# Output bias added by DMA from tile 2 on, and moves in VectorE's order, in a fused state-space and feed-forward layer

## The chip, the cores and the metric

The kernel runs on one core of one Trainium2 chip. The metric is the device time of one execution in microseconds; three runs of the kernel before took 1415.86, 1417.70 and 1417.96 us, so their median is 1417.7 us.

## The reference, cut to what matters

The input is x of 8192 rows by 512 columns, in float32. LN is a normalisation of each row without weights.

```
x = x + LN(attn(LN(x)))
x = x + LN(ffn(LN(x)))

attn(r):  u, v = split(r @ in_w + in_b);  v = conv3(silu(v)) + conv_b
          h_t = a*h_(t-1) + b*v_t;  y = c*h + d*v            (a scan over all 8192 rows)
          h = (u*silu(y)) @ out_w + out_b + r                (out_b: the output bias)
          return LN(h)*ln_w + ln_b
ffn(r):   W1, W2 rounded to -1, 0, 1
          return gelu(r @ W1 + b1) @ W2 + b2                 (2048 wide inside)
```

## The kernel before, in words

The rows are cut into 16 tiles of 512, each of four blocks of 128 rows (index j). Step s of a software pipeline works on four tiles at once: the feed-forward of tile fa = s-2, the second half of attention of tile c = s-1, the first half of attention of tile n = s+1, and the end of tile e = s-3. Steps 0 to 2 are the start-up, written out by hand; `for s in LATER` runs steps 3 to 17. Matmul operands are split into a high and a low float16 part, and each projection is three matmuls. For tiles 2 to 12 (`seven(t)`), the second matrix of the feed-forward uses seven half-width products in place of eight. These need differences of weight blocks (`combined`, made by eight calls of `combine(q, g)` in step 3) and, for each pair of chunks, four sums of the low parts (`presums`, L969 to L976, on VectorE).

The engines' queues are in order, and every order is written by hand: a list of (position, work) pairs is sorted by position and emitted by `run`. The names AT_... hold positions. A position of j means about "beside chunk j of the feed-forward" (16 chunks in a step, nine in the first half and seven in the second). What the step does on each engine:

- TensorE: `f1` of chunks 0 to 8 with `f2` four chunks behind, then `in_proj("u", c)` of four blocks (L579 to L581), three `f2`, `o(c, j)` of four blocks (L593 to L595), `in_proj("v", n)` of two blocks, the other `f1` and `f2`, and two more blocks of v. The u, o and v groups take turns in two PSUM banks (`misc`), so each group waits until the reader of the group before last is done: `gate` for u, `h_add` for o, `silu_v` for v. The first v group of a step also waits for the four transposing DMAs of x1T (L471), which SyncE issues once `t_lo("t1", n, j)` is done.
- VectorE: the ending of tile e (`epilogue`: additions `f_add` L938, statistics `f_stats` L907, `aggr` L917), `taps`, `scan` L1088, `y` L1098, `lo` L925 and `presums`. Then the four `gate` (L1120), statistics of x, `gate_lo`, `t_lo` (L1133), `h_add` (L1144), and the normalisations of tile c (`norms`).
- ScalarE: `gelu` L1855, `hi` L1869, `ffn_norm(e, j)` L1880 (it waits for GpSimd's `rstd_f(e)`, L2292 to L2324, which waits for the `aggr` of tile e), `silu_y` L1921, `gate_hi`, and then for each j `front(n, j)` and `residual(c, j)` L1916. The last writes the normed x into hb.
- GpSimd: the small vectors of each normalisation, `finish(e, j)` L2339 (a DMA that adds a block to the output in device memory), `keep_state`, and `add_bias(c, j)` L2349: it waits for `residual(c, j)` and adds the bias row to hb. `h_add(c, j)` waits for this and adds the product of the out projection.

The diff touches the positions at the top, `epilogue`, `h_add`, the loop body of VectorE, one line of ScalarE's loop and `add_bias`.

Of the kernel before, what the change touches and what calls it, by code (L numbers as in the profile page):

```python
# [24 lines left out]
P = 128  # L25
# [28 lines left out]
AT_F_ADD, AT_F_STATS, AT_F_AGGR = 0.0, 0.8, 1.15  # L54
AT_F_NORM = (4.15, 4.2, 5.15, 5.2)
AT_TAP0, AT_TAP2 = (1.1, 1.15, 1.4, 1.45), (1.3, 1.35, 2.25, 2.26)
AT_SCAN, AT_Y = (2.3, 2.35, 3.4, 3.45), (3.3, 3.35, 4.3, 4.35)
AT_LO = (1.2, 2.2, 2.32, 2.38, 3.36, 4.2)
AT_D_CONV, AT_CENTRE = (3.15, 3.16, 4.15, 4.16), (13.3, 13.5, 14.3, 14.5)
AT_NORMS, AT_NORMS_LAST = 7.7, 0.5  # L60
# [11 lines left out]
AT_TAP0_NEXT = (17.41, 17.42, 17.43, 17.44)  # L72
AT_PRESUM, AT_PRESUM_LAST = .005, .01
AT_F_STATS_SEVEN = 2.27
AT_F_NORM_SEVEN = (6.15, 6.2, 7.15, 7.2)
AT_COMBINED = (7.65, 9.25, 11.65, 14.65, 17.5)
LAG_END = 5
TH = TT // 2
AT_V = (8.9, 8.95, 16.3, 17.2)
# [16 lines left out]
def spread(at, step, works):  # L96

    return [(at + step * i, w) for i, w in enumerate(works)]


def build(nc, x, w_in, w_out, w1t, w2t, params, rows, out):
# [20 lines left out]
    def seven(t):  # L122

        return 1 < t < NT - 3
# [19 lines left out]
    with ExitStack() as ctx:  # L144
# [3 lines left out]
        def sem(name):  # L148
            return ctx.enter_context(nc.semaphore(name))
# [106 lines left out]
        out_st = [sem(f"out_st{i}") for i in range(NB)]  # L256
        x1_st = [sem(f"x1_st{i}") for i in range(NB)]
        last_st = [sem(f"last_st{i}") for i in range(NB)]

        const_ok, prep, pmx, pm1, scale_ok = sem("const_ok"), sem("prep"), sem("pmx"), sem("pm1"), sem("scale_ok")  # L260
        win_h, win_l, wo_h, wo_l = sem("win_h"), sem("win_l"), sem("wo_h"), sem("wo_l")
# [629 lines left out]
        def _(ve_):  # L891
# [17 lines left out]
            def aggr(ln, t, j):  # L909
                ve_.wait_ge(bn_ok[ln], NB * t + j + 1)  # L910
                if ln == 0 and t in (1, 2):
                    ve_.wait_ge(front_rs, min(j, 2) + 1 if t == 1 else NB + j // 2)
                elif ln == 0 and t > 2:
                    ve_.wait_ge(rs_ok[0], t - 2)
                elif t > 0:
                    ve_.wait_ge(rs_ok[ln], t)
                ve_.bn_aggr(mean_var(ln)[:, j, :], raw_stats(ln)[:, j, :]).then_inc(mv_ok[ln], 1)  # L917
# [11 lines left out]
            def f_add(e, j):  # L929
                if e == NT - 1 and j >= 2:  # L930
                    ve_.wait_ge(f2_sum, j - 1)
                elif j % 2 == 0:
                    ve_.wait_ge(f2_mm, half_done(e, j // 2))
                if e + 1 < NT - 1:
                    ve_.wait_ge(x3_lo, NB * (e + 1) + j + 1)
                else:
                    ve_.wait_ge(out_st[j], 16 * e)
                ve_.scalar_tensor_tensor(out=hb[:, j, :], in0=f2b[j][:, :], scalar=f_inv[:, 0:1], in1=b2_row,  # L938
                                         op0=ALU.mult, op1=ALU.add).then_inc(f_ok, 1)

            def f_stats(e, j):
                ve_.wait_ge(f_ok, NB * e + j + 1)
                stats(4, e, j, fo(e, j))
# [93 lines left out]
            def epilogue(e):  # L1037
                if seven(e):
                    return (spread(AT_F_ADD, .1, drain(e, 1))
                            + spread(AT_F_STATS_SEVEN, .001, [lambda j=j: f_stats(e, j) for j in range(2, NB)])  # L1040
                            + spread(AT_F_STATS_SEVEN + .004, .001, [lambda j=j: aggr(4, e, j) for j in range(2, NB)]))
                return (spread(AT_F_ADD, .2, [lambda j=j: f_add(e, j) for j in range(NB)])
                        + spread(AT_F_STATS, .1, [lambda j=j: f_stats(e, j) for j in range(NB)])
                        + spread(AT_F_AGGR, .01, [lambda j=j: aggr(4, e, j) for j in range(NB)]))

            def x_stats(n, j):

# [87 lines left out]

            def h_add(c, j):
                ve_.wait_ge(o_mm, NB * c + j + 1)
                if c > 0:
                    ve_.wait_ge(resb_ok, NB * (c - 1) + j + 1)
                else:  # L1140
                    ve_.wait_ge(x1_hi, j + 1)
                    ve_.wait_ge(wo_sc_ok, 2)
                dst = hb_of(c)[:, j, :]
                ve_.scalar_tensor_tensor(out=dst, in0=bank("o", c, j)[:, :], scalar=o_inv[:, 0:1],  # L1144
                                         in1=dst, op0=ALU.mult, op1=ALU.add).then_inc(h_ok, 1)
# [575 lines left out]
            for s in LATER:  # L1721
# [17 lines left out]
                    continue  # L1739
                if c is not None and c > 0:  # L1740
                    gate(c, 0)
                    gate(c, 1)
                if s == 3:
                    combine(2, 0)
                if n is not None:
                    run(ln1(n))
                if s == NT - 1:
# [9 lines left out]
                parts = drain(fa, 0) if seven(fa) else []  # L1757
                if n is not None:
                    if s == 3:
                        combine(0, 0)  # L1760
                    t_lo("t1", n, 0)
                    if s == 3:
                        combine(0, 1)
                    t_lo("t1", n, 1)
                    for part in parts[:3]:
                        part()
                    t_lo("t1", n, 2)
                    h_add(c, 0)
                    for part in parts[3:4]:
                        part()  # L1770
                    t_lo("t1", n, 3)
                    parts = parts[4:]
# [27 lines left out]
                    items = norms(c)  # L1800
                if s == 3:
                    b2_difference()
                    items += [(at, lambda i=i: combine(*divmod(i, 2))) for i, at in zip((2, 3, 5, 6, 7), AT_COMBINED)]
                if s < NT - 1:
                    items += [(at, lambda b=b: taps(s, b, True)) for b, at in enumerate(AT_TAP0_NEXT)]
                if fa is not None:
# [37 lines left out]
        def _(act):  # L1844
# [32 lines left out]
            def ffn_norm(e, j):  # L1877
                if j == 0:
                    act.wait_ge(rs_ok[4], e + 1)
                act.activation(fo(e, j), fo(e, j), ACT.Identity, bias=nm4[:, j:j + 1],  # L1880
                               scale=rs4[:, j:j + 1]).then_inc(fn_ok, 1)
# [345 lines left out]
            for s in LATER:  # L2227
                fa, c, n, e = tiles(s)
                items = []
                if e is not None:  # L2230
                    items += [(at, lambda j=j: ffn_norm(e, j)) for j, at in enumerate(AT_F_NORM_SEVEN if seven(e) else AT_F_NORM)]
                if c is not None and s < NT:
                    items += [(at, lambda b=b: d_conv(c, b)) for b, at in enumerate(AT_D_CONV)]
                if fa is not None:
                    items += ffn(fa, range(half(s)))
                if s == NT:
                    items += [(at, lambda j=j: t_hi("t3", c, j)) for j, at in enumerate(AT_T3_HI_LAST)]
                if s == NT + 1:
                    items += [(at, lambda j=j: last_norm(j)) for j, at in enumerate(AT_FIRST_LAST_NORM)]
                run(items)  # L2240
                if s >= NT:
                    continue
                for b in range(KC):
                    silu_y(c, b)
                if s == NT - 1:
                    centre_tap(NT - 1, 0)
                    centre_tap(NT - 1, 1)
                for b in range(KC):
                    gate_hi(c, b)
                    if s == NT - 1 and b < 2:  # L2250
                        centre_tap(NT - 1, 2 + b)
                for j in range(NB):
                    if n is not None:
                        front(n, j)
                    residual(c, j)
                if s == NT - 1:
                    for b in range(KC):
                        d_conv(NT - 1, b)
                    for j in range(NB):
                        residual(NT - 1, j)  # L2260
                items = ffn(fa, range(half(s), FC)) if fa is not None else []
                if n is not None:
                    items += [(at, lambda b=b: silu_v(n, b)) for b, at in enumerate(AT_V)]
                if s < NT - 1:
                    items += [(at, lambda b=b: centre_tap(s, b)) for b, at in enumerate(AT_CENTRE)]
                if c is not None:
                    items += [(at, lambda j=j: t_hi("t3", c, j))
                              for j, at in enumerate(AT_T3_HI if s < NT - 1 else AT_T3_HI_PAIR)]
                if s == NT - 1:
                    items += [(AT_SILU_LAST, lambda b=b: silu_y(NT - 1, b)) for b in range(KC)]  # L2270
                    items += [(AT_GATE_HI_LAST, lambda b=b: gate_hi(NT - 1, b)) for b in range(2)]
                run(items)
                if s == NT - 1:
                    for b in range(2, KC):
                        gate_hi(NT - 1, b)
# [4 lines left out]
        def _(pool):  # L2280
# [65 lines left out]
            def add_bias(c, j):  # L2346
                pool.wait_ge(res_ok, NB * (c - 1) + j + 1)
                dst = hb_of(c)[:, j, :]
                pool.tensor_tensor(dst, dst, ob_row, ALU.add).then_inc(resb_ok, 1)  # L2349

            def edges(n):

# [173 lines left out]
```

## Time and profile before

| What | Value |
|---|---|
| Runs | 1415.86, 1417.70, 1417.96 us |
| The profiled execution's own time | 1419.9 us |
| Its span, first to last instruction | 1418.1 us |
| TensorE busy | 1391.3 us (98% of the span) |
| VectorE, ScalarE, GpSimd busy | 1210.6, 911.7, 369.4 us |
| Mean granted TensorE clock | 0.997 |

Busy time is the union of the intervals in which an engine executed something. "Idle before" a row is the idle time of that engine right ahead of it, and the arrow tells which instruction's signal ended it. The profiled execution's own time is 1.8 us over its span, and 2.2 us over the median of the runs.

### The profile page before, as it was taken

The numbers are of one execution on the slowest core, as the hardware profiler recorded it, in microseconds if no ns is written. First come the engines' busy times: TensorE is split into PE (matmuls) and PEld (weight loads), VectorE is DVE, ScalarE is ACT, GpSimd is POOL, SyncE is SP. The second block draws the span as 40 slices with busy tenths as digits, with TensorE's granted clock in tenths as the row PEclk, the third lists the DMA queues.
The fourth block names the chain that finished last, engine by engine and source line by source line (L and its number), as shares of the span: only waits on it lengthen the run. The fifth ranks groups of instructions, "written<-read, shape, count | busy, mean of one in ns | idle before, by whom it ended". The sixth has DMA issues, their size and how long they took to land.

```text
span 1418.1 us, 24900 instructions
## 1 busy us (share of the span) xinstructions
PE 1391.3 (98%) x8954; PEld 878.9 (62%) x8954; DVE 1210.6 (85%) x2360; ACT 911.7 (64%) x1504; POOL 369.4 (26%) x522
## 2 busy tenths in 40 slices
PE   6999999999999999999999999999999999999997
PEld 4444556657667575666757667575676757555664
DVE  7999988978889898898988889898898988898534
ACT  7998565656757566666656757566666656854543
POOL 4234142321312213132231312214122231313111
PEclk9999999999999999999999999999999999999999
DMA  8713431513305133141332315133041332202320
GB/s 230 254 51 79 116 80 25 120 30 81 55 16 119 31 90 60 21 99 31 97 53 68 63 21 119 30 90 60 16 105 31 91 59 60 31 1 60 60 31 31
DMA packets 164652, 98.12 MB, mean 69 GB/s; under 512 B 133680, under 2 KB 133680, under 8 KB 164400
## 3 DMA queue, kind: packets, MB, share of 16 engines
q1 hardware_dynamic: 155888, 80.79, 22.8%
q0 software_dynamic: 8640, 15.73, 8.1%
q8 instruction: 71, 1.16, 0.3%
q14 instruction: 53, 0.43, 0.1%
HBM read 31.49 MB, written 32.51 MB: 45 GB/s over the span
## 4 chain that ended last, share of the span: by engine, by line
PE 52%; DVE 21%; issue 12%; ACT 4%; POOL 3%; DMA 0%; DVEq 0%; ACTq 0%; POOLq 0%
PE f1b L617 6%; PE f1b L616 6%; PE misc L581 5%; PE misc L580 5%; PE misc L579 5%; PE f2b L667 4%; DVE ring L925 4%; PE f2b L657 4%; DVE vl L1079 3%; PE misc L593 3%; PE misc L595 3%; PE misc L594 3%; PE f2b L640 3%; PE f2b L642 3%; DVE bn L907 2%
## 5 line engine op out<-in xcount | busy, mean ns | idle before, releaser
L616 PE MATMUL f1b<-x3T,w 128*128 128x256 f16 x1792 | 399.1, 273 | 0.0
L617 PE MATMUL f1b<-x3T,w 128*128 128x256 f16 x1792 | 399.0, 273 | 0.0
L1855 ACT ACTIVATE ring<-f1b,par 128x256 f32<-128x256 f32 x480 | 201.4, 471 | 212.5 <-PE f1b L617 212.2
L2292 POOL TENSOR_SCALAR ve<-mv 128x4 f32<-128x4 f32 (+2 forms) x89 | 46.5, 523 | 764.3 <-DVE mv L917 764.3
L925 DVE SCALAR_TENSOR_TENSOR ring<-ring,f_sc 128x512 f16<-128x512 f32 x256 | 187.2, 737 | 60.2 <-ACT ring L1869 60.1
L616 PEld LDWEIGHTS f1b<-x3T,w 128*128 128x128 fp8e5 x1792 | 175.7, 98 | 25.0 <-issue 0.4
L617 PEld LDWEIGHTS f1b<-x3T,w 128*128 128x128 fp8e5 x1792 | 175.6, 98 | 24.4
L1869 ACT ACTIVATE ring<-ring,f_sc 128x512 f16<-128x512 f32 x256 | 182.2, 719 | 0.0
L657 PE MATMUL f2b<-w,ring 128*128 128x512 fp8e5 x704 | 180.7, 379 | 0.0
L579 PE MATMUL misc<-x1T,win_hi 128*128 128x512 f16 x456 | 172.8, 379 | 0.0
L581 PE MATMUL misc<-x1T,win_lo 128*128 128x512 f16 x456 | 172.8, 379 | 0.0
L580 PE MATMUL misc<-x1T,win_hi 128*128 128x512 f16 x456 | 172.8, 379 | 0.0
L1984 ACT ACTIVATE vb<-misc,par,inv_sig 128x512 f32<-128x512 f32 x54 | 41.9, 776 | 116.2 <-PE misc L581 116.0
L907 DVE BATCH_NORM_STATS2 bn<-hb 128x6 f32<-128x512 f32 x162 | 104.7, 677 | 0.2
L2349 POOL TENSOR_TENSOR hb<-hb,row 128x512 f32<-128x512 f32 x56 | 79.7, 1425 | 91.4 <-ACT hb L1916 91.4
L657 PEld LDWEIGHTS f2b<-w,ring 128*128 128x128 f16 x704 | 68.9, 98 | 50.2
L640 PE MATMUL f2b<-w,ring 128*128 128x512 fp8e5 x256 | 97.0, 379 | 0.9 <-DVE ring L925 0.8
L642 PE MATMUL f2b<-w,ring 128*128 128x512 fp8e5 x256 | 97.0, 379 | 0.0
L1079 DVE SCALAR_TENSOR_TENSOR vl<-vb,par,vl 128x512 f32<-128x512 f32 x128 | 92.4, 769 | 1.0 <-POOL vb L2398 0.8
L593 PE MATMUL misc<-wo_hi,g_hi 128*128 128x512 f16 x240 | 91.0, 379 | 2.2 <-DVE hb L1144 1.8
L594 PE MATMUL misc<-wo_lo,g_hi 128*128 128x512 f16 x240 | 91.0, 379 | 0.0
L595 PE MATMUL misc<-wo_hi,g_lo 128*128 128x512 f16 x240 | 91.0, 379 | 0.0
(263 smaller groups left out, 2693.5 us busy)
## 6 DMA issues: line engine op xcount, KB each, us to landing
out_dram<-xs SPq DMA_DIRECT2D x60, 256.0 KB, 3.0
xs<-x_dram SPq DMA_DIRECT2D x14, 1024.0 KB, 5.9
out_dram<-hb POOLq DMA_DIRECT2D x38, 256.0 KB, 5.3
out_dram<-stage POOLq DMA_DIRECT2D x22, 256.0 KB, 4.7
ring<-w1t_dram SPq DMA_DIRECT2D x3, 1024.0 KB, 13.4
stage<-w2t_dram SPq DMA_DIRECT2D x3, 1024.0 KB, 7.9
x1T<-tp SPq DMA_TRANSPOSE x68, 3.1
xs<-x_dram SPq DMA_DIRECT2D x4, 256.0 KB, 3.5
```

The lines of the kernel that those rows point to most:

```text
L579: pe.matmul(o[:, :], wh, x1T[:, s_, k, :], start=k == 0, stop=False)
L580: pe.matmul(o[:, :], wh, x1T[:, s_, KC + k, :], start=False, stop=False)
L581: mm = pe.matmul(o[:, :], wl, x1T[:, s_, k, :], start=False, stop=k == KC - 1)
L616: pe.matmul(o_, w, src[:, k, h * TH:(h + 1) * TH], start=k == 0, stop=False)
L617: mm = pe.matmul(o_, w, src[:, KC + k, h * TH:(h + 1) * TH], start=False, stop=k == KC - 1)
L640: pe.matmul(f2b[q][:, :], h_hi[:, i % H_SLOTS, qs], w2[:, chunk, :], start=chunk == 0, stop=False)
L642: mm = pe.matmul(f2b[q][:, :], h_lo[:, i % H_SLOTS, qs], w2[:, chunk, :], start=False, stop=chunk == FC - 1)
L657: pe.matmul(f2b[q][:, :], h_hi[:, r, n * TH + q * P:n * TH + (q + 1) * P], w2[:, chunk, :], start=p == 0 and n == 0, stop=False, skip_grou ...
L925: ve_.scalar_tensor_tensor(out=h_lo[:, i % H_SLOTS, :], in0=gg[:, i % G_SLOTS, :], scalar=f_sc[:, 0:1], in1=h_hi[:, i % H_SLOTS, :], op0=A ...
L1079: ve_.scalar_tensor_tensor(out=dst, in0=src, scalar=w, in1=dst, op0=ALU.mult, op1=ALU.add).then_inc(done, 1)
L1855: ins = act.activation(gg[:, i % G_SLOTS, ts], f1b[i % 2][:, ts], ACT.Gelu, bias=par[:, B1 + chunk:B1 + chunk + 1], scale=1.0 / ACT_SCALE)
L1869: act.activation(h_hi[:, i % H_SLOTS, :], gg[:, i % G_SLOTS, :], ACT.Copy, scale=f_sc[:, 0:1]).then_inc(hh_ok, 1)
```

## The change

From tile 2 on, `add_bias` no longer adds on GpSimd. GpSimd issues a DMA that reads the bias row from device memory for all 128 partitions and adds it to the block in hb, and `h_add` waits for the landing of this DMA, by new semaphores `ob_in`. Tile 1 keeps the addition on GpSimd.

In VectorE's order: `scan` of block 3 moves from position 3.45 to 4.25 in every step. The eight `combine` of step 3 move up by one place each, so that none is left at position 17.5. In the one step whose tile e comes right before the tiles of the seven products (step 4, e = 1), the statistics of tile e move from 0.8 to 2.4, and ScalarE's `ffn_norm` of this tile from the positions 4.15 to 5.2 to the positions 6.15 to 7.2.

```diff
-AT_SCAN, AT_Y = (2.3, 2.35, 3.4, 3.45), (3.3, 3.35, 4.3, 4.35)
+AT_SCAN, AT_Y = (2.3, 2.35, 3.4, 4.25), (3.3, 3.35, 4.3, 4.35)
...
+AT_F_STATS_NEXT = 2.4
...
-AT_COMBINED = (7.65, 9.25, 11.65, 14.65, 17.5)
+AT_COMBINED = (7.65, 9.25, 11.65, 14.65)
...
+        ob_in = [sem(f"ob_in{i}") for i in range(NB)]
...
+                at = AT_F_STATS_NEXT if seven(e + 1) else AT_F_STATS
                 return (spread(AT_F_ADD, .2, [lambda j=j: f_add(e, j) for j in range(NB)])
-                        + spread(AT_F_STATS, .1, [lambda j=j: f_stats(e, j) for j in range(NB)])
-                        + spread(AT_F_AGGR, .01, [lambda j=j: aggr(4, e, j) for j in range(NB)]))
+                        + spread(at, .1 if at == AT_F_STATS else .001, [lambda j=j: f_stats(e, j) for j in range(NB)])
+                        + spread(at + .004 if seven(e + 1) else AT_F_AGGR, .01 if at == AT_F_STATS else .001,
+                                 [lambda j=j: aggr(4, e, j) for j in range(NB)]))
...
             def h_add(c, j):
                 ve_.wait_ge(o_mm, NB * c + j + 1)
-                if c > 0:
-                    ve_.wait_ge(resb_ok, NB * (c - 1) + j + 1)
+                if c > 1:
+                    ve_.wait_ge(ob_in[j], 16 * (c - 1))
+                elif c == 1:
+                    ve_.wait_ge(resb_ok, j + 1)
...
                 if c is not None and c > 0:
                     gate(c, 0)
+                    if s == 3:
+                        combine(2, 0)
                     gate(c, 1)
                 if s == 3:
-                    combine(2, 0)
+                    combine(0, 0)
...
                     if s == 3:
-                        combine(0, 0)
+                        combine(0, 1)
                     t_lo("t1", n, 0)
                     if s == 3:
-                        combine(0, 1)
+                        combine(1, 0)
                     t_lo("t1", n, 1)
...
-                    items += [(at, lambda i=i: combine(*divmod(i, 2))) for i, at in zip((2, 3, 5, 6, 7), AT_COMBINED)]
+                    items += [(at, lambda i=i: combine(*divmod(i, 2))) for i, at in zip((3, 5, 6, 7), AT_COMBINED)]
...
-                    items += [(at, lambda j=j: ffn_norm(e, j)) for j, at in enumerate(AT_F_NORM_SEVEN if seven(e) else AT_F_NORM)]
+                    items += [(at, lambda j=j: ffn_norm(e, j)) for j, at in enumerate(AT_F_NORM_SEVEN if seven(e) or seven(e + 1) else AT_F_NORM)]
...
             def add_bias(c, j):
                 pool.wait_ge(res_ok, NB * (c - 1) + j + 1)
                 dst = hb_of(c)[:, j, :]
-                pool.tensor_tensor(dst, dst, ob_row, ALU.add).then_inc(resb_ok, 1)
+                if c == 1:
+                    pool.tensor_tensor(dst, dst, ob_row, ALU.add).then_inc(resb_ok, 1)
+                    return
+                if c > 2:
+                    pool.wait_ge(ob_in[j], 16 * (c - 2))
+                pool.dma_start(dst, rows[0:1, :].partition_broadcast(P)[:, 0, :], accum_op=ALU.add).then_inc(ob_in[j], 16)
```

## Rows read from the trace of the kernel before

**Rows 1.** The page, part 1: busy us, share of span, instructions.
```profile
PE 1391.3 (98%) x8954; PEld 878.9 (62%) x8954; DVE 1210.6 (85%) x2360; ACT 911.7 (64%) x1504; POOL 369.4 (26%) x522
```

**Rows 2.** TensorE's waits: line, releaser, us in total, times, longest.
```profile
PE f2b L667 <- DVE stage L969: 2.6, 1, 2.6
PE misc L593 <- DVE hb L1144: 1.8, 1, 1.8
```

**Rows 3.** Timeline of VectorE, turn to step 4: start us, us, line, idle before.
```profile
259.08 1.22 DVE L955 TENSOR_TENSOR stage<-w,stage 128x1024 fp8e5<-128x1024 fp8e5 x1
...
262.85 2.46 DVE L907 BATCH_NORM_STATS2 bn<-hb 128x6 f32<-128x512 f32 x4
```

**Rows 4.** Timeline of TensorE: the first f2 of step 4, and of step 6.
```profile
265.74 1.03 PE L657 MATMUL f2b<-w,ring 128*128 128x512 fp8e5 x4
269.32 0.52 PE L667 MATMUL f2b<-w,ring 128*128 128x256 fp8e5 x2 [2.56 <-DVE stage L969]
...
273.51 1.03 PE L657 MATMUL f2b<-w,ring 128*128 128x512 fp8e5 x4
...
440.54 1.03 PE L657 MATMUL f2b<-w,ring 128*128 128x512 fp8e5 x4
...
443.91 1.03 PE L657 MATMUL f2b<-w,ring 128*128 128x512 fp8e5 x4
```

**Rows 5.** Windows: stretch, length, busy by engine, granted clock, DMA share, GB/s.
```profile
268.00:274.00 6.00, 4.67 (x26) 3.37 (x27) 5.93 (x11) 4.56 (x9) 2.70 (x5) 0.72 0.31 42
126.00:130.00 4.00, 3.16 (x15) 1.48 (x16) 4.00 (x11) 0.54 (x2) 2.79 (x5) 1.00 0.67 245
```

**Rows 6.** Timelines of step 6: the ending of tile 3, and the first gate.
```profile
443.29 0.30 DVE L917 BATCH_NORM_AGGREGATE mv<-bn 128x2 f32<-128x6 f32 x2
...
447.43 0.27 POOL L2324 TENSOR_SCALAR nm<-tmp 128x4 f32<-128x4 f32 x1
...
448.26 1.41 DVE L1098 SCALAR_TENSOR_TENSOR yb<-vl,cb_par,yb 128x512 f32<-128x512 f32 x2
...
448.83 1.51 ACT L1880 ACTIVATE stage<-stage,nm,rs 128x512 f32<-128x512 f32 x2
451.12 0.84 ACT L1855 ACTIVATE ring<-f1b,par 128x256 f32<-128x256 f32 x2 [0.78 <-PE f1b L617]
...
459.13 0.75 DVE L1120 SCALAR_TENSOR_TENSOR yb<-misc,bu_sig,yb 128x512 f32<-128x512 f32 x1 [0.35 <-ACT yb L1921]
...
461.10 0.38 PE L579 MATMUL misc<-x1T,win_hi 128*128 128x512 f16 x1
```

**Rows 7.** Timelines of step 6: bias additions, `h_add`, out projection, first v block.
```profile
470.31 1.27 POOL L2349 TENSOR_TENSOR hb<-hb,row 128x512 f32<-128x512 f32 x1 [3.07 <-ACT hb L1916]
477.00 1.28 POOL L2349 TENSOR_TENSOR hb<-hb,row 128x512 f32<-128x512 f32 x1 [0.95 <-ACT hb L1916]
...
481.72 0.75 DVE L1144 SCALAR_TENSOR_TENSOR hb<-misc,o_inv,hb 128x512 f32<-128x512 f32 x1
...
476.34 0.38 PE L593 MATMUL misc<-wo_hi,g_hi 128*128 128x512 f16 x1
...
481.52 0.38 PE L579 MATMUL misc<-x1T,win_hi 128*128 128x512 f16 x1
```

**Rows 8.** DMA views, 440 to 465 us: software queue, landings of adding DMAs.
```profile
q0 software_dynamic: 576, 1.05, 30.2%
...
out_dram<-stage POOLq DMA_DIRECT2D x2, 256.0 KB, 4.6
```

**Rows 9.** DMA views, 465 to 490 us: hardware queue, transposes, last issue.
```profile
q1 hardware_dynamic: 4224, 1.05, 26.5%
...
x1T<-tp SPq DMA_TRANSPOSE x4, 3.1
...
476.97 1.23 SPq L471 DMA_TRANSPOSE x1T<-tp  x1
```

**Rows 10.** The page, part 6: plain loads of 1 MB.
```profile
xs<-x_dram SPq DMA_DIRECT2D x14, 1024.0 KB, 5.9
```

## The prediction

> **What bounds the kernel now.** I read the page's first part, then TensorE's waits, then timelines of the two places where the change could bite. TensorE is busy in 1391.3 of 1418.1 us [rows 1], so only a change in what TensorE waits for moves the time. All its waits in the steady part come to one entry: 2.6 us, once, until a VectorE sum (L969) is done [rows 2]. The other one shown, 1.8 us, lies in the start-up at 126 us, which the change doesn't touch. The reader is to see where the 2.6 us lie: at 265.74 us TensorE starts the first f2 of step 4, and it goes on only at 269.32 [rows 4]. From this f2 to the next one takes 273.51 - 265.74 = 7.77 us; the same stretch of step 6 takes 443.91 - 440.54 = 3.37 us. So this place costs 4.40 us, more than the wait: the granted clock is 0.72 in 268 to 274 us [rows 5], full speed for a part and half for the rest, so after the wait TensorE ran at 1.2 GHz for a while. The 1.8 us wait left the clock at 1.00 in 126 to 130 us [rows 5]. I keep this pair: waits of 1.8 us cost themselves, one of 2.6 us cost 1.7 us more.
>
> **The moves around step 4.** Ahead of these sums VectorE's list has a combine at 259.08 (1.22 us, some 1.13 to the next start) and four statistics with four aggr (2.46 us for the four, 2.7 with the aggr) [rows 3]. Both go elsewhere: 1.13 + 2.7 = 3.8 us sooner. The wait is 2.6, so it goes whole, and the clock's part with it: -4.40 us. What is late next there is ScalarE's hi, on which the same sums depend in step 6 too, and step 6 has no such wait [rows 4]. The combine that leaves this place pushes each of the others one place up in step 3, where nothing of TensorE's waits (no wait of step 3 is in rows 2); the first goes between two gates, where VectorE waits for TensorE. I price it at nothing; were that cover gone it would be 1.2 us, once.
>
> The four statistics now come after the sums of pair 2, 3. In step 6 these end at 448.26 [rows 6], and there two statistics of the ending tile (half of 2.7, some 1.4 us) are ahead of them; in step 4 they end on that clock at 448.26 - 1.4 = 446.9, and the statistics at 449.6. In step 6 the last aggr ends at 443.6 and GpSimd's chain at 447.7, 4.1 us later [rows 6]. So in step 4 the chain ends at 453.7, and ScalarE, which comes to ffn_norm at 448.83, waits 4.9 us. Behind this instruction are queued two gelu and three hi (ScalarE has slack there: the gelu at 451.12 waits 0.78 us for TensorE [rows 6], and I allow 1.5 us in all), then silu_y, then VectorE's first gate. The gate would move some 3.4 us from 459.13, to end at 463.3; TensorE's third u group, at 461.10 [rows 6], needs its bank. That gives a new wait of up to 2.2 us; if GpSimd's chain and the slack turn out 1 us kinder it is 1.1. I take 1.6 us. A bound below is none at all, above 2.6 with the clock's 1.7 on top, 4.3. Net of step 4: -4.40 + 1.6 = -2.8 us, with ends -4.4 and 0.
>
> The scan of block 3 goes behind the sums of pair 4, 5 in each step. Those get 1.2 us sooner; TensorE doesn't wait for them in step 6 (no entry in rows 2), and y of block 3, which needs the scan, stays where it was with the same work ahead. Nothing, from -0.2 to +0.2 us a step (a bound from the 0.3 us of one such sum).
>
> **The adding DMAs.** In step 6 the additions on GpSimd run from 470.31 to 478.28, 1.27 us each [rows 7]. VectorE adds the out projection after each; TensorE didn't wait there. GpSimd has nothing urgent behind them, so their removal is worth nothing. In their place come four DMAs of 256 KB a step, issued the first at about 470.3, the last at about 477.0 [rows 7], the others evenly between. The same kind of DMA towards device memory lands 4.6 us after its issue [rows 8]. The first would land at 474.9, h_add(0) end at 475.7, and its bank is wanted at 476.34 [rows 7]: just in time. The fourth would land at 481.6, beside the 481.72 at which h_add(3) starts now. Alone, the DMAs fit.
>
> They aren't alone. In the same 7 us SyncE issues the four transposing DMAs of x1T, the last at 476.97, landing 3.1 us later at 480.1 [rows 9], and TensorE's first v block at 481.52 [rows 7] waits for all four: 1.4 us of slack. The work of all 16 DMA engines: four adding DMAs take 30.2% of 25 us = 7.5 us [rows 8], four transposes 26.5% of 25 us = 6.6 us [rows 9]. First packets come about 1.2 us after the first issue, at 471.5. One after the other the two streams end at 471.5 + 14.1 = 485.6, 4.1 us after TensorE wants v. That is the upper end. The lower end: a plain load of 1 MB takes 5.9 us with its latency [rows 10], at most 1.5 us per 256 KB, and with some 2 us of latency off about 1.0; then 471.5 + 4.0 + 5.3 (the 6.6 less one hiccup, since their landings of 3.1 with 1.2 of start leave little more than 1.3 to 1.7 each) = 480.8, in time. An adding DMA into SBUF reads two operands and writes one, so I take 1.4 us each, between the plain load and the 1.9 measured towards device memory: 471.5 + 5.6 + 5.3 = 482.4, and the last landing at 482.5. Which stream is last decides where it hurts. Transposes move 4224 small packets, the adds 576 [rows 8, 9]; if the engines take turns, an add's large packets go ahead and the transposes end last. Then v waits 482.5 - 481.5 = 1.0 us. This holds in steps 3 to 14, which have both streams: 12 x 1.0 = +12 us, with ends 0 and 12 x 4.1 = 49 us. In step 15 there are no x1T transposes; nothing.
>
> The Trainium skill (DMA: Bandwidth & Descriptors, section Queues, rings and completion order) says that each DMA engine goes round between its queues a packet of descriptors at a time; by that rule the transposes are last, as I have it, and no row of before has both queues at work to show it. The same page (Anatomy of one DMA) fits a DMA issued by GpSimd as 2.0 us and bytes over 436 GB/s, an estimate of 2.6 us for 256 KB; by it the adds would be hidden. The trace disagrees for adding DMAs, with 4.6 us [rows 8], and I go by the trace.
>
> **Sum.** The profiled execution took 1419.9 us, 1.8 over its span and 2.2 over the median of the runs. 1419.9 - 2.8 + 12 = 1429.1, less 2.2: 1427 us.
>
> **Rivals.**
> 1. The adds are hidden. Adding into SBUF costs the engines about 1.0 us each, or both streams overlap in the engines; the last transpose lands before 481.5. For it: alone each landing is in time to a few tenths. Against it: the engines' measured shares add up to more than the time there is. It decides below 1.15 us a DMA, where the streams end at 481.4. Then only step 4 counts: 1417.7 - 2.8 = 1414.9 us, not slower.
> 2. The transposes go first, and the adds are last. The fourth add lands at 482.5 to 484; h_add(3) then ends at 483.3 to 484.8, and its bank is wanted by the second v block 2.6 us after 481.52, at 484.1. h_add(2) is similarly late for the first v block. About 0.7 us a step, 13 steps with tile 14: 1417.7 - 2.8 + 9 = 1424 us.
> 3. The wait gets long enough for the clock to fall: 2.7 us a step and the 1.7 us of rows 4 with it: 12 x 4.4 = 53, 1417.7 - 2.8 + 53 = 1468 us. For it: the upper end of the sum; against it, it needs adds at the full 1.9 us.
>
> **How the numbers follow.** A measurement of this kernel can tell 0.2%, 2.8 us. Forecast, 0.42: waits of 0.3 to 2.3 us a step, 1418.5 to 1442.5 us; nearly all slower. Rival 1, 0.38: its time lies on the edge of 0.2%; by what step 4 gives back I split it 0.26 faster and 0.12 within. Rival 2, 0.11, of which 0.02 within. Rival 3, 0.09. With 0.03 of the forecast within 0.2%: faster 0.26, within 0.17, slower 0.57. Range 1413 to 1445 us; it leaves out rival 3 and the tails. The forecast's own range is 1418.5 to 1442.5.
>
> **What would show it.** Right: L667's 2.6 us gone from TensorE's waits, and no clock under 1.00 near 270 us; a wait of ScalarE for GpSimd's chain of some 5 us in step 4, and of 1 to 2 us for a gate behind it; TensorE waiting about 1 us before L579 in steps 3 to 14, put down to the transposes; their landings at 4 to 5.5 us in place of 3.1. Wrong: landings of transposes still at 3.1 and of adds at 4.6 or less (rival 1); waits put down to L1144 (rival 2); a granted clock under 1.00 once a step (rival 3); the 4.9 us of ScalarE absent.

## The result and the profile after

The changed kernel took 1470.6 us (median of 4 runs, 1466.77 to 1480.28) against 1417.3 us before (median of four, one run more than the three behind 1417.7): ratio 1.039, 95% interval 1.037 to 1.041. I had forecast 1427 us with a range of 1413 to 1445, so the sign was right and the size wrong by a factor of more than five. The profiled execution has a span of 1465.0 us, 46.9 more than before.

Line numbers moved by a few: f2's half products are L669 now (L667 before), u and v L581 to L583 (L579 to L581), o L595 (L593), h_add L1150 (L1144), gate L1124 (L1120), the bias DMA L2362 (the addition was L2349). First the page, part 1, and TensorE's waits (line, releaser, us in total, times, longest), beside [rows 1, 2].

```profile
PE 1400.9 (96%) x8954; PEld 876.9 (60%) x8954; DVE 1202.2 (82%) x2360; ACT 911.9 (62%) x1504; POOL 347.2 (24%) x522
```

```profile
PE misc L595 <- DVE hb L1150: 23.7, 20, 2.7
PE misc L581 <- DMA x1T<-tp: 20.1, 12, 3.9
PE f1b L707 <- ACT tp L1967: 7.8, 1, 7.8
PE misc L581 <- DVE yb L1124: 1.8, 1, 1.8
```

Two entries carry the loss, all of them in the steady part, where before had neither: 20 waits for h_add and 12 for the transposes, 43.8 us. 1.8 us is a new gate wait in step 4; the 2.6 us for L667 are gone. The 1.8 us for h_add in the start-up [rows 2] are gone too, though nothing there was changed; e5's trace has such a wait of 1.7 us again, so it isn't the change's doing. With the small ones, all waits that the view lists grew from 17.5 to 56.7 us, by 39.2.

TensorE's busy time grew by 9.6 us for the same 8954 matmuls. About half is the clock, which fell to half at some of the waits (mean 0.995, before 0.997). Each fall lasts 3.4 us in the clock's record and so costs 1.7; there are four in the steady part after, one before, so 5.1 us more. The rest is, by my estimate, the ends of matmuls: a row of 512 columns takes 0.38 us and the next starts 0.21 us behind it (481.17 and 481.38 us in the trace after), so each of nearly 30 more waits leaves some 0.17 us that no next matmul overlaps. 39.2 and 9.6 us, less 1.8 by which the stretch behind the last matmul is shorter, make the 46.9 us.

Now part 3 (queue, packets, MB, share of 16 engines over the span) and the DMA issues (line, count, KB, median us to landing).

```profile
q1 hardware_dynamic: 155888, 80.79, 24.4%
q0 software_dynamic: 16704, 30.42, 14.9%
...
hb<-rows_dram POOLq DMA_DIRECT2D x52, 256.0 KB, 7.1
...
x1T<-tp SPq DMA_TRANSPOSE x68, 5.7
```

GpSimd's queue took 14.9% of 1465 us in place of 8.1% of 1418: 218 - 115 = 103 us more for 56 adding DMAs, 1.85 us of all 16 engines each. These shares count the time in which packets stand open, so with two queues open they can add up to more than the engines' time (2.43 in a window below). SyncE's queue moved the same bytes in 24.4% of 1465 = 357 us in place of 22.8% of 1418 = 323 us: its packets stood open longer. The adds land after 7.1 us, the transposes of x1T after 5.7 in place of 3.1 [rows 9].

Step 6 shows how. Timelines of GpSimd, VectorE and TensorE, beside [rows 7]:

```profile
480.54 0.95 POOL L2362 DMA_DIRECT2D hb<-rows_dram  x1 [3.29 <-ACT hb L1924]
...
487.25 0.86 POOL L2362 DMA_DIRECT2D hb<-rows_dram  x1 [1.37 <-ACT hb L1924]
...
484.04 0.69 DVE L1137 SCALAR_TENSOR_TENSOR tp<-xn,tp 128x512 f16<-128x512 f32 x1 [0.37 <-ACT tp L1967]
488.11 0.75 DVE L1150 SCALAR_TENSOR_TENSOR hb<-misc,o_inv,hb 128x512 f32<-128x512 f32 x1 [3.38 <-DMA hb<-rows_dram]
488.78 0.47 DVE L997 SCALAR_TENSOR_TENSOR stage<-f2b,f_inv,stage 128x256 f32<-128x256 f32 x1
489.17 0.68 DVE L1137 SCALAR_TENSOR_TENSOR tp<-xn,tp 128x512 f16<-128x512 f32 x1
...
488.92 0.39 PE L595 MATMUL misc<-wo_hi,g_hi 128*128 128x512 f16 x1 [2.41 <-DVE hb L1150]
498.05 0.38 PE L581 MATMUL misc<-x1T,win_hi 128*128 128x512 f16 x1 [2.09 <-DMA x1T<-tp]
```

The first add lands 7.5 us after its issue, h_add(0) waits 3.38 us for it, and TensorE's third o group waits 2.41 us for the bank. The fourth t_lo is queued behind h_add on VectorE: it starts at 489.17, 5.1 us behind the third, where it was 2.2 behind. So the fourth transpose is issued late as well (on the mean of steps 6 to 14 the last is issued 7.9 us behind the first, in place of 6.7), and then v waits 2.09 us for it. Windows of the same stretch (length, busy of each engine, granted clock, DMA share, GB/s):

```profile
485.30:487.30 2.00, 1.21 (x6) 0.36 (x4) 0.00 (x0) 1.62 (x3) 0.63 (x2) 1.00 1.22 47
487.30:491.50 4.20, 2.58 (x9) 1.07 (x10) 1.97 (x4) 0.00 (x0) 0.81 (x1) 0.81 1.12 152
491.90:493.90 2.00, 2.00 (x8) 0.77 (x7) 1.97 (x4) 0.00 (x0) 0.00 (x0) 0.65 2.43 37
```

The reader is to see the last two columns: in the first and the last window the DMA engines have more than their whole time in open packets (of both queues at once) and move only 37 to 47 GB/s, between them 152. The records hold transposing packets of 256 bytes that stood open for up to 2.6 us there; in step 6 of before the longest is 1.2 us.

### The profile page after: what moved, and what is told of

The parts are those of the page before. It is cut to its first block, busy times and chain, and to the rows that moved or that the text cites. A ratio compares the mean times of both kernels' runs of the same rounds, so it can differ in the third digit from the quotient of the medians.

```text
span 1465.0 us, 24952 instructions
## 1 busy us (share of the span) xinstructions
PE 1400.9 (96%) x8954; PEld 876.9 (60%) x8954; DVE 1202.2 (82%) x2360; ACT 911.9 (62%) x1504; POOL 347.2 (24%) x522
## 3 DMA queue, kind: packets, MB, share of 16 engines
q1 hardware_dynamic: 155888, 80.79, 24.4%
q0 software_dynamic: 16704, 30.42, 14.9%
## 4 chain that ended last, share of the span: by engine, by line
PE 40%; DVE 19%; issue 15%; DMA 11%; ACT 4%; POOL 4%; DVEq 0%; POOLq 0%; ACTq 0%
PE f1b L619 7%; PE f1b L618 7%; DMA x1T<-tp 6%; DMA hb<-rows_dram 4%; PE misc L581 4%; PE misc L583 4%; PE misc L582 4%; DVE ring L927 4%; PE f2b L642 4%; PE f2b L644 4%; DVE vl L1083 3%; DVE bn L909 3%; PE f2b L669 2%; PE f2b L659 2%; POOL rsc L2301 1%
## 5 line engine op out<-in xcount | busy, mean ns | idle before, releaser
L581 PE MATMUL misc<-x1T,win_hi 128*128 128x512 f16 x456 | 173.5, 381 | 21.8 <-DMA x1T<-tp 20.1
L583 PE MATMUL misc<-x1T,win_lo 128*128 128x512 f16 x456 | 173.4, 380 | 0.0
L595 PE MATMUL misc<-wo_hi,g_hi 128*128 128x512 f16 x240 | 92.8, 387 | 24.0 <-DVE hb L1150 23.7
L581 PEld LDWEIGHTS misc<-x1T,win_hi 128*128 128x128 f16 x456 | 44.8, 98 | 78.8 <-issue 27.2
L1150 DVE SCALAR_TENSOR_TENSOR hb<-misc,o_inv,hb 128x512 f32<-128x512 f32 x56 | 41.9, 747 | 60.0 <-DMA hb<-rows_dram 57.0
```

The source lines that it names most:

```text
L581: pe.matmul(o[:, :], wh, x1T[:, s_, k, :], start=k == 0, stop=False)
L583: mm = pe.matmul(o[:, :], wl, x1T[:, s_, k, :], start=False, stop=k == KC - 1)
```

## The experiments

**The two halves of the change.** e1 is the changed kernel with GpSimd's additions back, e2 the kernel before with the adding DMAs.

```diff
 e1_moves: add_bias and h_add as before, all else as changed
 e2_adds:  add_bias and h_add as changed, all orders as before
```

> The moves in VectorE's and ScalarE's orders alone; GpSimd adds the bias as before. If the prediction's step on the moves holds: L667's wait of 2.6 us and the half clock near 270 us are gone, a gate wait of about 1.75 us stands in step 4, net -2.6 to -2.8 us (ratio 0.998). Rival: the moves have a part in the loss, through the scan that goes later in each step; then the time is above 1417 us.

> The adding DMAs alone, orders as before. If they carry the whole loss: 1470.6 + 2.7, some 1473 us (ratio 1.039 to 1.042), with about 20 us of waits for the transposes and 24 us for h_add. Rival, that the moved scan or combines made it worse: clearly under 1465 us.

e1: 1414.15 us against 1416.06 before in the same job, ratio 0.9986 (0.9977 to 0.9995). e2: 1476.2 us, 1.0435 (1.0412 to 1.0457). The adds carry the whole loss (e2's interval touches the change's, so that they carry more is not shown); the moves bring 2 us. e2's trace has 22.1 us of waits for the transposes and 24.0 for h_add, as expected. TensorE's waits of e1:

```profile
PE misc L581 <- DVE yb L1124: 1.7, 1, 1.7
PE f2b L642 <- DVE ring L927: 0.8, 1, 0.8
```

No L669 any more, and the gate wait of 1.7 us that stands in its place, as forecast. The scan that goes later in each step costs nothing: TensorE has no other wait in any steady step (the 0.8 us lie behind them, at 1267 us).

**Is it the chain from issue to h_add, or the meeting of two streams?** e3 has e1's additions on GpSimd and issues beside each an adding DMA of the same size into output rows of the last tile, which are stored over at the end; in the steady part nothing waits for it.

```diff
+                if 1 < c < NT - 1:
+                    pool.wait_ge(...)   # this block's DMA of the tile before
+                    pool.dma_start(out_d[NT - 1, j], ob_row, accum_op=ALU.add).then_inc(ob_in[j], 16)
                 pool.tensor_tensor(dst, dst, ob_row, ALU.add).then_inc(resb_ok, 1)
```

> The moves, GpSimd's additions, and beside each of tiles 2 to 14 an adding DMA of 256 KB from SBUF to rows of the output that are stored again at the end; nothing in the steady part waits for it. Theory A (the two DMA streams get in each other's way): transposes land at 4 to 6 us in place of 3.1, TensorE waits 10 to 30 us for them in all, 1425 to 1445 us, and no h_add waits. Theory B (only the chain of issue, landing and h_add is too long): transposes unhurt, 1415 to 1418 us.

1471.0 us, 1.0371 (1.0333 to 1.0408): the same loss though no h_add waits for a DMA. Theory A holds, but its number was too low, and "no h_add waits" was wrong.

```profile
PE misc L585 <- DMA x1T<-tp: 24.7, 10, 3.7
...
PE misc L599 <- DVE hb L1152: 6.5, 12, 2.6
PE misc L585 <- DVE hb L1152: 4.6, 2, 2.4
```

The mean clock is 0.989 here: in all steps but the first of the 12 one wait has 2.1 to 3.7 us, and at six of them the clock falls to half. The 11.1 us for h_add come from GpSimd, which issues a DMA (0.9 us) before each of its additions. That also makes the last transpose late, issued 8.6 us behind the first in place of 6.7 (mean of steps 6 to 14). The last landing comes at 14.3 us in place of 9.7. So some 2 of these 4.6 us are e3's own delay and not the meeting of the streams; e4 below is freer of it.

e5 is e3 with the four DMAs issued behind `rstd(1, c)`, when x1T's transposes have landed.

```diff
                     rstd(1, c, rsc[:, 0, :], True)
+                    for j in range(NB):
+                        shadow(c, j)        # e3's DMA, taken out of add_bias
```

> As e3_shadow, but GpSimd issues the four adding DMAs of a step some 7 us later, behind the scale of the out projection's normalisation, when the transposes of x1T have landed and those of x3T are 25 us away. If the loss is the meeting of the two streams: the time of e1_moves, 1414 us within 3, transposes land at 3.1. If the extra 13 MB or GpSimd's work of issuing cost something by themselves: over 1425 us.

1417.0 us, 1.0007 (0.9998 to 1.0016), transposes at 3.1 us. The same 13 MB at another time of the step cost some 3 us over e1, not 57, and in the traces 2.7 of them lie behind the last matmul (10.6 us in place of 7.9). The place in time is the cause; what e3 and e5 leave open is the part of GpSimd's issuing, which e5 moves as well. Alone, the four adding DMAs of a step have this share of 25 us (window of 480 to 505 us in e5's trace; packets, MB, share), 1.71 us each:

```profile
q0 software_dynamic: 576, 1.05, 27.3%
```

**Adding, or any DMA?** e4 is the changed kernel with the DMA writing plainly in place of adding; e6 has that plain DMA on SyncE's queue, e9 on ScalarE's. In all three the bias overwrites the residual.

```diff
 e4: -pool.dma_start(dst, ..., accum_op=ALU.add)
     +pool.dma_start(dst, ...)
 e6: the same DMA issued by sp, behind transpose("t1", n, j)
 e9: the same DMA issued by act, behind residual(c, j)
```

> The changed kernel with the same DMAs from the bias row, but writing plainly instead of adding (so hb holds the bias in place of residual plus bias). If it is the work of 16 engines that counts, a plain load takes about 0.8 to 1.0 us of them in place of 1.7 to 2.0, and half or more of the loss goes: 1418 to 1440 us. If any DMA of GpSimd's queue beside the transposes does the harm, whatever it does: 1460 us or more.

> As e4_plain (the bias row written plainly over hb by DMA, so residual is left out), but SyncE issues each load on its own queue, behind the transpose of its block. The same bytes, engines and landing time. If it is two queues at work at once that hurt the transposes: 1414 to 1420 us. If it is copies and transposes at once in the same engines, by whichever queue: 1445 us or more. By the share of work alone (5.3 + 4 x 0.7 to 0.9 us from 471.5 on, over by 481) 1414 to 1418 us too, but then e4_plain's 1464 stays unexplained.

> As e4_plain and e6_sp_plain (the bias row written plainly over hb, residual left out), but ScalarE issues each load, behind its residual: a second queue beside SyncE's, of the hardware kind, not GpSimd's software kind. Issuing and waiting holds ScalarE some 0.5 us a block, so the last t_hi and transpose come 1.5 to 2 us later and v would wait 0.3 to 1 us a step for that alone: 1418 to 1427 us if only GpSimd's software queue hurts the transposes, with transposes landing at 3.1 to 4. If any second queue does: landings of 5 to 6 us and 1450 us or more.

e4 took 1463.9 us (1.0336), e6 1423.5 us (1.0058), e9 1431.2 us (1.0109). Of each, the waits for the transposes and the landings:

```profile
PE misc L581 <- DMA x1T<-tp: 26.6, 12, 4.3
PE misc L595 <- DVE hb L1150: 8.4, 13, 1.4
...
hb<-rows_dram POOLq DMA_DIRECT2D x52, 256.0 KB, 5.9
...
x1T<-tp SPq DMA_TRANSPOSE x68, 6.0
```

```profile
PE misc L609 <- DVE xs L1164: 4.8, 1, 4.8
...
PE misc L595 <- DMA x1T<-tp: 1.1, 1, 1.1
...
hb<-rows_dram SPq DMA_DIRECT2D x52, 256.0 KB, 4.0
...
x1T<-tp SPq DMA_TRANSPOSE x68, 3.8
```

```profile
PE misc L581 <- DMA x1T<-tp: 14.2, 11, 2.1
...
hb<-rows_dram ACTq DMA_DIRECT2D x52, 256.0 KB, 3.5
...
x1T<-tp SPq DMA_TRANSPOSE x68, 4.4
```

The fences are e4, e6, e9 in this order. The same bytes into the same place cost 50 us of TensorE's time on GpSimd's queue, and next to nothing in the steady steps on SyncE's own. There the 4.8 us is one wait for tile 15, whose loads stand behind other work in that queue by my making, with a fall of the clock behind it; without the two (4.8 and 1.7 us) e6 would be at some 1417 us, in the expected range, my estimate. In e4 GpSimd has less to do than before and the last transpose is issued only 0.5 us late, but the last landing comes 14.0 us after the first issue in place of 9.7 (e6: 11.1). So the transposes are slowed without any delay by GpSimd.

My guess that a plain load costs 1.0 us of the engines failed on GpSimd's queue: 13.2% of 1461 less 115 us is 78 us, 1.4 us each. On ScalarE's queue it holds: e9's page has 4.2% of 1429 = 60 us for its 56 loads, 1.07 each. One thing beside the queue differs in e6: each load stands behind the transpose of its block, and the last load lands about 1 us behind the last transpose; in e4 it is the last transpose that lands behind.

On ScalarE's queue the harm is small but there: landings of 4.4, not the 5 to 6 of "any second queue", and 14.2 us of waits in 11 steps. The last landing comes 12.5 us after the first issue in place of 9.7, of which 1.1 us is late issue (the last transpose is issued 7.7 us behind the first in place of 6.7, as ScalarE is held up). So neither of my two cases for e9 is right as put; its time lies above the one and far below the other.

**How it goes with the bytes and with the source.** e7 adds 256 of the 512 columns, e11 16 of them (the others are left without bias); e12 reads the bias from its copy in SBUF.

```diff
 e7:  dst[:, 0:TH] <- rows[0:1, 0:TH]
 e11: dst[:, 0:16] <- rows[0:1, 0:16]
 e12: pool.dma_start(dst, ob_row, accum_op=ALU.add)
```

> The changed kernel with the adding DMAs over the left 256 columns only (the bias of the right half is left out): half the bytes in the same number of DMAs and packets. If the loss goes with the engines' time: waits about halve or better, 1425 to 1440 us. If it goes with the meetings of the streams, whatever their size: 1455 to 1470 us.

> The changed kernel with the adding DMAs over 16 of 512 columns (the bias of the other columns is left out): the same number of DMAs and descriptors on GpSimd's queue, 1/32 of the bytes. If the delay of the transposes goes with the bytes (9.7 us from first issue to last landing without adds, 11.9 with half, 14.3 with all of them): 9.7 to 10.2 and the time of e1_moves, 1413 to 1416 us. If GpSimd's queue costs by itself: landings over 4 us and 1420 us or more.

> The changed kernel with the adding DMAs reading the bias from its copy in SBUF in place of the row in device memory. If the reads of one row of device memory by 128 descriptors are slow: adds of 1.4 us of the engines in place of 1.9 and 1430 to 1455 us. If the adding itself or the queue is: 1465 to 1475 us as before.

| Kernel | Bytes a DMA | Time, ratio | x1T: first issue to last landing, mean of 9 steps |
|---|---|---|---|
| before | none | 1416 to 1417, 1 | 9.7 us |
| e11 | 8 KB | 1413.2, 0.9979 (0.9970 to 0.9988) | 10.8 us |
| e7 | 128 KB | 1426.1, 1.0075 (1.0057 to 1.0093) | 12.1 us |
| e12 | 256 KB, from SBUF | 1456.2, 1.0290 (1.0252 to 1.0327) | 14.0 us |
| after | 256 KB, from device memory | 1470.6, 1.039 | 15.4 us |

The last column is from the trace's issues and landings (steps 6 to 14). The DMAs' number alone costs 1.1 us (I expected at most 0.5), which the slack of some 1.5 us hides, so e11 is as fast as e1. The slack is used up between 8 and 128 KB; from there each microsecond goes to TensorE, and more where the clock falls: less 1.5 us and times 12, the delays are 11, 34 and 50 us, and over e1 the kernels lose 12, 42 and 56. Reading from SBUF saves a quarter of the loss (and e12's waits for h_add fell to 4.5 and 3.8 us), so the source is a part of it, not the cause. e12 lies between my two cases, and its adds cost 1.74 us each (14.6% of 1453.5 less 115), not 1.4.

**A better version.** e8 is e1 with ScalarE's `ffn_norm` of tile 1 one place later; e10 is e8 with the scan back.

```diff
 e8:  +AT_F_NORM_NEXT = (7.15, 7.2, 8.15, 8.2)      # for seven(e + 1) in place of (6.15, 6.2, 7.15, 7.2)
 e10: -AT_SCAN = (2.3, 2.35, 3.4, 4.25)
      +AT_SCAN = (2.3, 2.35, 3.4, 3.45)
```

> e1_moves with ScalarE's four ffn_norm of tile 1 one place later again (7.15, 7.2, 8.15, 8.2). ScalarE then waits about 1.2 us for GpSimd's chain in place of 4.8, silu_y moves some 1.9 us against step 6 in place of 3.4, and the gate wait of step 4 falls from 1.73 to 0.2 to 0.7 us: 1413 us, 1.0 to 1.5 us under e1_moves. If the wait goes elsewhere (f1's gelu): no gain.

> e8_late_norm with the scan of block 3 back at 3.45. In the steady steps nothing should change. In step 4 the four statistics are now ahead of the sums of pair 4, 5, and the 1.2 us of the scan would bring these some 0.7 us behind f2's need: one wait for L971 of 0.5 to 0.9 us and 1413.5 us, up to 1 us over e8_late_norm. If the scan's place does nothing even there: no wait, same time.

e8 took 1412.8 us, 0.9977 (0.9968 to 0.9987), faster than the kernel before and than the change; its interval overlaps e1's, so that it beats e1 is shown by the trace only, where the gate wait is 0.4 in place of 1.7 us. e10 took 1414.0 us, 0.9987 (0.9978 to 0.9996), by its interval not to be told from e8. Its trace has the wait that I expected:

```profile
PE misc L582 <- DVE yb L1125: 0.6, 1, 0.6
PE f2b L670 <- DVE stage L972: 0.5, 1, 0.5
```

## Why the prediction was wrong

**The moves: the mechanism right, the gain smaller.** I had -4.40 + 1.6. The 2.6 us and the half clock at 270 us are gone; ScalarE waits 4.82 us for GpSimd's chain (forecast 4.9), and the gate wait is 1.75 (forecast 1.6, 1.1 to 2.2). The rows of ScalarE and TensorE after:

```profile
281.42 1.52 ACT L1888 ACTIVATE hb<-hb,nm,rs 128x512 f32<-128x512 f32 x2 [4.82 <-POOL nm L2332]
```

```profile
268.00:274.00 6.00, 6.00 (x50) 4.62 (x48) 5.93 (x11) 5.22 (x11) 0.00 (x0) 1.00 0.06 19
```

e1 measured -1.9 us (between 0.7 and 3.3 by its interval) for -2.8. A reason for less, not tested by itself: the clock's 1.7 us at this place were not always lost. e2 has the orders of before and waits 2.4 us there, and its clock stays at 1.00:

```profile
PE f2b L668 <- DVE stage L970: 2.4, 1, 2.4
```

```profile
268.00:274.00 6.00, 4.47 (x37) 3.63 (x38) 5.93 (x11) 6.00 (x12) 2.84 (x5) 1.00 0.29 25
```

The scan's new place costs nothing in the steady steps, and e10 shows what it is for.

**The adding DMAs: the mechanism right, the size wrong in two terms.** The step that failed is "I take 1.4 us each". Measured: 1.85 us, in the changed kernel, 1.71 in e5 towards device memory with no transpose beside them, 1.6 for tile 15's four into SBUF (35.1% of 18 us) beside two transposes, next to the 1.9 that [rows 8] gave for adding DMAs towards device memory. I had that number, and argued it down from a plain load that goes by SyncE's queue; e4 shows that even a plain load costs 1.4 us on GpSimd's. The second term is the transposes' own work: 6.6 us a step by [rows 9], which I cut to 5.3. Beside the adds their queue's share grew besides, by 34 us over the run, 2.8 a step.

With the rows as they stood, 7.5 and 6.6 us, the sum is my upper end, the two streams one after the other: the last landing at 485.6, 15.3 us after the first issue. Measured are 15.4 us; part of this agreement is luck, as 1.3 us of it come from the last transpose's late issue, which the sum had not. TensorE's waits for the two are 43.8 us, 3.7 for each of 12 steps, under the 4.1 of that end. The loss of the adds, 1470.6 less e1's 1414.2, is 56 us, 4.7 a step: the falls of the clock and the ends of matmuls come on top of the waits, and the forecast had no term for them.

**The rivals were not exclusive.** I made "transposes last" and "adds last" two cases with a price each. Both came true in the same step, as h_add's delay pushes the fourth t_lo and its transpose back too. e4 has most of h_add's waits away (8.4 us in place of 23.7) and keeps 50 of the 56 us, as TensorE waits longer for the transposes (26.6 us in place of 20.1). So slower transposes suffice for most of the loss, and taking away the waits for h_add brings little.

**The clock.** Rival 3 gave 1468 us, close to what came, but its mechanism (one wait of 2.7 us and 1.7 of clock in each step) isn't what the trace shows: the clock fell after four of 32 steady waits. By waits and not by clock, 39 of 47 us. It is e3 that comes nearest to rival 3, with the clock at half in six steps. I gave that case 0.09 because it "needs adds at the full 1.9 us"; by the only measured row for an adding DMA, that was the likeliest value.

The last transpose lands 0.1 to 1.0 us behind the last add in each of the 12 steps. The Trainium skill's rule that I named (DMA: Bandwidth & Descriptors, Queues, rings and completion order: an engine goes round between its queues) agrees with this order. The Trainium skill's fit (same page, Anatomy of one DMA), by which I estimated 2.6 us for 256 KB from GpSimd, is not what the trace has, even with little else under way: tile 15's four adds begin to land after 4.2 us and follow each other by 1.7 us on the mean.

**What stays open.** Why the engines do so little in some stretches (37 to 47 GB/s) while both streams are open, and why GpSimd's queue harms the transposes so much more than ScalarE's with the same bytes. On SyncE's queue (e6) the order behind the transposes and the queue itself were not tested apart. No run here takes the descriptor traffic of GpSimd's queue apart from its data; e11 only bounds the part that doesn't go with bytes to 1.1 us a step.

## What to carry to other kernels

Before work is moved from an engine to DMA, look at what the DMA engines do in just that stretch, and add up their shares against the time to the first consumer of either stream: an average of a few per cent over the span says nothing, as e3 and e5 differ by 54 us with the same transfers. For an operation that the trace doesn't show, the nearest measured row is the value to take, and an argument why it should be cheaper belongs into the lower bound. And when two streams meet, price the case that both are late.

## What I had not expected of the hardware

- Four transposes on SyncE's queue and four adding DMAs on GpSimd's, issued in the same 7 us, were over 15.4 us after the first issue, about as late as one stream after the other (7.5 and 6.6 us of the engines by the rows of before). The share of SyncE's queue grew from 323 to 357 us, and single transposing packets of 256 bytes stood open for up to 2.6 us.
- A plain load of 256 KB costs the engines about 1.4 us on GpSimd's queue beside transposes (e4) and 1.07 on ScalarE's beside the same transposes (e9), against 0.8 at the 316 GB/s that a plain load of 1 MB on SyncE's queue alone reaches at 435 to 440 us in the trace of before.
- The length of a wait alone doesn't tell whether the clock falls: in the changed kernel it was at half after waits of 2.0, 2.4 and 2.5 us, and not after one of 2.66 us at 1030 us; at one and the same place it fell at a wait of 2.56 us in before and not at one of 2.39 in e2.
